# Two-layer AdaLN kernel on one core: modulation products in other pauses of TensorE, transposes between projection halves, gate floor on two rows, expert weights in another order

## The reference

```python
mod = (_silu(L0_c) @ L0_wmod).reshape(L0_c.shape[0], 6, 1, -1)
sa, ca, ga, sb, cb, gb = (mod[:, 0], mod[:, 1], mod[:, 2], mod[:, 3], mod[:, 4], mod[:, 5])
ga = (2 * (ga >= 0) - 1) * jnp.maximum(jnp.abs(ga), 0.25)
gb = (2 * (gb >= 0) - 1) * jnp.maximum(jnp.abs(gb), 0.25)
h = _layernorm(x, axis=-1) * (1 + ca) + sa
x = x + ga * _L0_attn_ref(h, ...)
h = _layernorm(x, axis=-1) * (1 + cb) + sb
x = x + gb * _L0_ffn_ref(h, ...)
...                      # layer 1 the same with its own weights
```

## Time and profile before

| | before |
|---|---|
| median of 3 runs | 437.23 us (436.45 to 443.87) |
| profiled execution | 439.2 us |
| its span, first to last instruction | 437.4 us, 6180 instructions |
| busy share of the span | PE 93%, PEld 70%, DVE 66%, ACT 46%, POOL 30% |
| mean granted TensorE clock | 0.968 of full (2.4 GHz) |
| DMA | 56.89 MB, mean 130 GB/s |

### The profile page before, as it was taken

The page is one execution under the profiler, slowest core; times in us unless marked ns, Lnnn a source line. Parts: engine busy times, 40 slices in busy tenths (PEclk is TensorE's granted clock), DMA queues, the critical chain, the costliest instruction groups (busy, mean ns, idle before and its releaser), DMA issues. The chain is left out here.

```text
span 437.4 us, 6180 instructions
## 1 busy us (share of the span) xinstructions
PE 406.4 (93%) x1923; PEld 305.2 (70%) x1924; DVE 288.4 (66%) x703; ACT 201.9 (46%) x380; POOL 129.3 (30%) x143
## 2 busy tenths in 40 slices
PE   6996898888999999999998899899999979999997
PEld 6553748445777777777776637787677858798887
DVE  4898886997444444444443465989685999985542
ACT  2578825382222222222222238382796488622430
POOL 1000020004777777777777500601000010010000
PEclk9999696988999999999999969999999999999999
DMA  7995766981323233333239249911500000001001
GB/s 262 415 399 132 154 152 178 354 374 43 102 97 104 100 108 96 105 97 109 96 107 275 85 164 377 352 42 25 191 1 0 1 1 0 2 1 45 4 0 49
DMA packets 24010, 56.89 MB, mean 130 GB/s; under 512 B 4528, under 2 KB 15794, under 8 KB 22996
## 3 DMA queue, kind: packets, MB, share of 16 engines
q1 hardware_dynamic: 18564, 41.80, 28.5%
q0 software_dynamic: 5424, 14.82, 10.3%
HBM read 46.10 MB, written 10.50 MB: 129 GB/s over the span
## 5 line engine op out<-in xcount | busy, mean ns | idle before, releaser
L736 PE MATMUL bank<-arena,tile_mem 128*128 x224 | 75.6, 460 | 0.0
L1411 POOL DMA_INDIRECT tile_mem<-h_dram,gidx x57 | 56.0, 982 | 53.8 <-DVE gidx L1789 36.7
L1399 POOL TENSOR_TENSOR rstd<-ve,mhalf 128x2 f32<-128x2 f32 (+1 forms) x14 | 11.3, 806 | 186.3 <-DVE ve L1539 186.3
L1418 POOL DMA_INDIRECT y_dram<-norm,didx x56 | 55.3, 988 | 22.4 <-issue 13.7
L1805 DVE TENSOR_TENSOR tile_mem<-tile_mem,bank 128x176 f32<-128x176 f32 x56 | 18.9, 337 | 62.6 <-ACT tile_mem L1209 62.6
L752 PE MATMUL bank<-arena,tile_mem 88*128 x224 | 57.7, 379 | 0.8 <-DVE tile_mem L1800 0.8
L752 PEld LDWEIGHTS bank<-arena,tile_mem 88*128 88x128 f32 x224 | 42.3, 190 | 15.8 <-issue 1.3
L736 PEld LDWEIGHTS bank<-arena,tile_mem 128*128 128x128 f32 x224 | 38.2, 190 | 11.9
L847 PE MATMUL bank<-x_r,f_r 128*128 128x512 f32 x192 | 44.9, 392 | 0.8 <-DVE x_r L1985 0.7
L1209 ACT ACTIVATE tile_mem<-bank 128x176 f32<-128x176 f32 x56 | 17.8, 317 | 57.8 <-PE bank L736 57.8
L1204 ACT ACTIVATE tile_mem<-bank 128x256 f32<-128x256 f32 x57 | 21.9, 384 | 44.9 <-PE bank L729 44.8
(11 more groups left out here) (286 smaller groups left out, 729.7 us busy)
## 6 DMA issues: line engine op xcount, KB each, us to landing
arena<-w_gu SPq DMA_DIRECT2D x3, 2112.0 KB, 12.4
arena<-w_dn SPq DMA_DIRECT2D x4, 1408.0 KB
arena<-w_gu SPq DMA_DIRECT2D x2, 2464.0 KB, 20.8
arena<-y_dram SPq DMA_DIRECT2D x6, 768.0 KB, 7.8
arena<-w_f SPq DMA_DIRECT2D x6, 512.0 KB, 7.8
arena<-wmod SPq DMA_DIRECT2D x3, 512.0 KB, 9.1
arena<-wmod SPq DMA_DIRECT2D x2, 768.0 KB, 10.8
arena<-y_dram SPq DMA_DIRECT2D x4, 384.0 KB, 4.8
```

The costliest lines, as they stand in the source:

```text
L736: mm = pe.matmul(bank[2 + r % 2][:, 0:2 * M], xgT[r % 2][:, k * P:(k + 1) * P], gu[:, bass.ds(e[k], 2 * M)], start=(k == 0), stop=(k == CT ...
L1411: pool.indirect_dma_start(out=xg[j % 4], out_offset=None, in_=h2_dram, in_offset=bass.IndirectOffsetOnAxis(ap=gidx[:, j:j + 1].bitcast(U32 ...
L1418: pool.indirect_dma_start(out=y_dram, out_offset=bass.IndirectOffsetOnAxis(ap=didx[:, j:j + 1].bitcast(U32), axis=0), in_=yt[j % 4], in_of ...
```

## The change

- The first two pieces of layer 1's modulation products stand behind the two `gated_weights`, the third behind `project(0)`. Their banks become 2, 5, 4, and their waits change with them. `mod_cols` of layer 1 stands ahead of `project(1)`, after a wait for the copy out of bank 2.
- `transposes(B, 0)`, the second norm of sequence 0, stands between the two halves of `project(1)`.
- ACT loads the sigmoid's table ahead of `keep_x(0)`, and `keep_x(1)` stands ahead of `modulated(3, ...)`.
- The floor of layer 0's second gate is applied to the two raw rows (2 x 256) on DVE right behind `exponents(2)`, before they are stored and broadcast, and no more on 128 x 512 ahead of the experts' loop. SP now waits for `gbraw_ready` 2.
- The gate and up weights of experts 17 to 31 are loaded right after `proj_done` reaches B, ahead of the stores of x and h2. Only experts 14 to 16, which lie on X, are loaded after both x stores.

The core of the diff:

```diff
-MOD_BANKS = 4, 7, 4
+MOD_BANKS = 2, 5, 4
...
+        PAST_X = EARLY + -(-NT * C // GUW)
...
-            sp_.wait_ge(gbraw_ready, 1)
+            sp_.wait_ge(gbraw_ready, 2)
             sp_.dma_start(modg_dram, gb_raw).then_inc(mod_out[0], 16)
...
             sp_.dma_start(dn[:, DN_LATE * DNW:E * DNW], w_dn[:, DN_LATE * DNW:E * DNW]).then_inc(dn_in, 16)
+            sp_.wait_ge(proj_done, B)
+            for e in range(PAST_X, E, 5):
+                sp_.dma_start(gu[:, e * GUW:(e + 5) * GUW], w_gu[:, e * GUW:(e + 5) * GUW]).then_inc(gu_late, 16)
...
             sp_.wait_ge(x1_out, 16 * B)
-            for e in range(EARLY, E, 6):
-                sp_.dma_start(gu[:, e * GUW:(e + 6) * GUW], w_gu[:, e * GUW:(e + 6) * GUW]).then_inc(gu_late, 16)
+            sp_.dma_start(gu[:, EARLY * GUW:PAST_X * GUW], w_gu[:, EARLY * GUW:PAST_X * GUW]).then_inc(gu_late, 16)
...
-                    pe.wait_ge(*((sig_ready, CT + 1), (sig_ready, CT + 2), (modrow_ready, 1))[n])
+                    pe.wait_ge(*((exparg_ready, CT + 1), (exparg_ready, CT + 2), (sig_ready, CT + 1))[n])
...
-            def project(b, banks):
+            def project(b, banks, between=None):
 
                 for t in range(TB):
+                    if t == 2 and between:
+                        between()
...
-            for b in range(B):
-                gated_weights(b)
+            gated_weights(0)
+            mod_rows(range(1))
+            gated_weights(1)
+            mod_rows(range(1, 2))
             pe.wait_ge(wg_ready, B)
             preload_x(0, RES_BANKS[0])
             pe.wait_ge(yT_ready, CT)
             project(0, RES_BANKS[0])
-            pe.wait_ge(exparg_ready, CT + 1)
+            mod_rows(range(2, 3))
+            pe.wait_ge(modrow_ready, 1)
             pe.wait_ge(v_used, CT + 1)
             preload_x(1, RES_BANKS[1])
-            mod_rows(range(3))
+            mod_cols((SA, CA, SB, CB), modrow1, 3, 4)
             pe.wait_ge(yT_ready, CT * B)
-            project(1, RES_BANKS[1])
-            mod_cols((SA, CA, SB, CB), modrow1, 3, 4)
+            project(1, RES_BANKS[1], lambda: transposes(B, 0, None, LN2_BANKS[0]))
             pe.wait_ge(route_in, 32)
             for b in range(B):
-                transposes(B + b, b, (x_done, b) if b else None, LN2_BANKS[b])
                 if b:
+                    transposes(B + b, b, (x_done, b), LN2_BANKS[b])
...
+            act.preload_act_table(ACT.Sigmoid)
             keep_x(0)
             modulated(2, 0, 0, SB, CB, LN2_BANKS[0])
...
             token_scores(0)
+            keep_x(1)
             modulated(3, 1, 0, SB, CB, LN2_BANKS[1])
...
             exponents(2)
+            dve.wait_ge(gbraw_ready, 1)
+            gate_floor(gb_raw, gb_tmp[0], gb_tmp[1], gbraw_ready, gb_raw)
             outputs(0)
...
-            dve.wait_ge(modB_in[0], 16 * B)
-            gate_floor(*[v.rearrange("p t c -> p (t c)") for v in (gb0[:, :, :], norm[:, TB:TB + 2, :], norm[:, TB + 2:NT, :])])
-            settle()
```

More of the change, by code:

```diff
@@ L187, in two_layers @@
         modrow1 = tile_mem[0:B, 0:6 * C]
-        gb_raw = tile_mem[0:B, 6 * C:7 * C]
+        gb_raw, *gb_tmp = [tile_mem[0:B, i * C:(i + 1) * C] for i in (6, 7, 8)]
         sh_hid = tile_mem[:, 0:SHT * S].rearrange("p (m n) -> p m n", m=SHT)
@@ L786, in _ @@
             pe.wait_ge(gu_early, 16 * 2)
-            pe.wait_ge(gu_late, 16 * 3)
+            pe.wait_ge(gu_late, 16 * 4)
             pe.wait_ge(dn_in, 16 * 4)
@@ L1153, in _ @@
             token_scores(1)
-            keep_x(1)
             token_rows(1)
@@ L1486, in mod_cols, with gate_floor @@
                 ins.then_inc(modcol_ready, 1)
-            def gate_floor(g, sign, size, done=None):
+            def gate_floor(g, sign, size, done=None, out=None):
                 step(stt(size, g, -1.0, g, ALU.mult, ALU.max))
@@ L1496, in gate_floor @@
                     return step(stt(g, sign, -1.0, size, ALU.add, ALU.mult))
-                stt(size, sign, -1.0, size, ALU.add, ALU.mult).then_inc(done, 1)
+                stt(size if out is None else out, sign, -1.0, size, ALU.add, ALU.mult).then_inc(done, 1)
             def norm_stats(t, src):
@@ L1912, in gated_sums @@
                 pair = slice(ts[0], ts[-1] + 1)
+                if ts[0] == 0:
+                    dve.wait_ge(modB_in[0], 16 * B)
                 dve.wait_ge(csum_done, ts[-1] + 1)
```

## The result

The change made the kernel slower. The median is 449.08 us (448.5 to 451.35, four runs) against 438.75 for the kernel before in the same comparison, a ratio of 1.0232 [1.0189, 1.0274]. The profiled execution took 448.65 us, with a span of 446.8 and a mean granted clock of 0.957 (before 437.4 and 0.968). The forecast was 446.5 us, which is 1.0212 of its base of 437.23, with a range of 443 to 450. The 449.08 lies 2.6 above it, and 1.5 of that is the base, 438.75 here.

The account below looks back on a forecast made before the run. The experts' loop start bounds the kernel, set by DVE's one-hot work, which would now wait for h2 stores behind weights. 8.4 + 0.9 = 9.3 us on 439.2 gives 448.5 profiled, 446.5 as median; range 443 to 450.

Parts of the forecast that it names:

- The first term: DVE's one-hot work waits for the second h2 store, landing at 96.05 instead of 87.6: 8.4 us later, range 7.0 to 10.8.
- The turn: SP's queue: down weights drained by 74.15 before, 2.2 us later after the change, so the moved weights start at 76.35.
- The step on the gate floor: The gate row's store starts at 34.2, lands 35.9; down weights go 2.2 us later, ends 1.2 and 4.2.
- The weights: SP's queue: three moved loads, 5.41 MB at 435 GB/s, take 12.4 us, to 88.75.
- The stores: Behind the weights, three stores take 1.4 us each, 4.2 in all, to 92.95; the second h2 store lands 3.1 later.
- the lower end, 94.6: Earliest landing of the second h2 store: down weights draining only 1.2 us later and 1.2 us for each store.
- The second term: One-hot stretch: TensorE idle about 88 to 97, so half clock at the first shared-expert piece, +0.9 us (-2.1 to +3.0).
- TensorE's order: Moved products and transposes: 2 us gained ahead of DVE's wait, or up to 4 lost at half clock; swallowed either way.
- The gate floor on DVE: Four added operations take 1.6 us in the 2.08 us pause ahead of 34.64; removing those behind `gidx` gives 0.
- 435: Rival: stores don't wait behind the weights, h2 lands before DVE comes, TensorE's 2 us are kept; 435 us, chance 0.08.
- 443.5: Rival: moved weights use the idle DMA share while down weights drain, 1.3 MB or 3.0 us; 443.5 us, chance 0.08.
- 452: Rival: half clock lasts into the experts' loop, doubling TensorE's 5.41 busy us of 104 to 112; 452 us, chance 0.06.

Follow-up runs that it names:

- w_only: The kernel before with only the weight loads of experts 17 to 31 moved ahead of the x and h2 stores; ratio 1.0206, span 446.0 us.
- w_back: The change with its weight loads back behind the x and h2 stores, all other parts kept; ratio 0.9977, span 438.4 us.
- one_load: The change with one weight load (experts 27 to 31, 1.80 MB) ahead of the stores instead of three; ratio 1.0040, span 438.8 us.
- stores_act: The change with both h2 stores issued from ACT's queue, weights still ahead on SP's; ratio 1.0272, span 451.5 us.
- w_back_busy: The change with weight loads behind the stores, plus unused TensorE products: 12 ahead of `project(1)`, two behind each one-hot group; ratio 0.9948, span 431.9 us.
- busy_gap2: The change with 47 unused matmuls in TensorE's wait for the h2 stores and two behind each group of six one-hot products; ratio 1.0217.

## Why the prediction was right, point by point

**The mechanism was right.** The h2 stores stood behind the weights, the wait that had 6.2 us to spare became the one that sets the loop's start, and the loop moved with it one for one. w_only shows that it suffices, w_back that nothing else is lost, as far as its interval tells, and one_load that it goes by bytes.

**The first term, 8.4, measured 8.6, but out of three sizes that were each off; that they nearly cancel is luck.**

- The turn. The step on the gate floor put the issue of the down weights 2.2 later. It came 1.2 later (35.81 against 34.60), as the step's lower end said: the floor ended at 33.77, and the loads followed the row's store by 1.16, less than the 1.7 that I took as the shortest landing. The down weights still ended 2.3 later than before, at 77.26. That is 0.9 behind the 76.35 of the sum. Where the other 1.1 of the 2.3 come from is not shown; in w_only, without the floor, they ended 1.1 later than before too.
- The weights. From there they took 91.2 - 77.26 = 13.9 us, not 12.4, though 0.89 of their 5.41 MB had gone before. The rate was not far off, 420 GB/s in 78 to 88 instead of 435, but rows of the stores ran among theirs from 85.02 on.
- The stores. In return they needed 96.4 - 91.2 = 5.2 us behind the weights, not 4.2 + 3.1 = 7.3; the first of them landed 0.4 after the last weights.

Together +0.9 + 1.5 - 2.1 = +0.3, which puts 96.05 at 96.4. So "one behind the other, each in its time alone" is too sharp: all the bytes together set the end, and the rows mix. Two numbers under it were off as well. The twin store with the 2.7 us was not issued into an empty queue: the first h2 store, issued at 75.25, landed after 3.2, at 78.45, and so ran beside it. And the lower end, 94.6, adds up to 94.5.

The landings keep the order of issue: the weights at 91.2, the second h2 store at 96.4. That agrees with the rule that the forecast went by, in the Trainium skill ("DMA: Bandwidth & Descriptors", section "Queues, rings and completion order"), that each DMA engine takes its descriptors in ring order. The trace does not name the engine of a row, so the order within one engine is not seen.

**The second term, +0.9 for half clock at the first piece, measured +0.94** in DVE's wait and +1.0 in the whole stretch. The place was as put: the first piece took 2.91 instead of 1.98, the second 2.91 as before, the third pair 2.98 where it took 2.84.

**TensorE's order.** The gain of 2 us measured 2.0 (DVE's cast ahead of the wait stands at 85.53 instead of 87.57, the logits 1.56 earlier), and the wait swallowed it, as the step said. Two sizes inside were off. The second projection began 1.5 earlier, at 58.71, not 0.2: with the modulation products in TensorE's pauses, its clock in 42 to 49 was 1.00 instead of 0.63, the first projection began at 47.06 instead of 48.88, and DVE's last output came 1.4 earlier. Against that the half of the projection took 3.78, not 1.86, at the lower clock behind a pause of 2.96; that was the other end that the step named, and it was covered. In w_back, where the cover is gone, the order leads by 2.9 at the one-hot work.

**The gate floor on DVE.** It took 1.36 us (1.6 forecast) in the pause ahead of 34.6, of which 0.80 was left, and the removal behind `gidx` gave nothing: DVE is idle for 3.71 there, the 1.32 of before and 2.4 more.

**The rivals.** The stores waited, so 435 fell; and stores_act shows that not even a queue of their own gives it. The weights did use the idle share, with 0.89 MB ahead of the down weights' end (1.3 MB in the rival), but the second h2 store landed no earlier for it, so 443.5 fell. The loop began at full clock after the change (1.00 in 115.3 to 119.3, and its copies keep their 9.5 to tile 50), so 452 fell here, though in w_back the half clock does reach into the loop, for 1.1 us. Its working has a slip: 5.41 busy us of 8 in 104 to 112, a stretch that is not among rows 7, leave TensorE idle for a third of the time, not for half.

**The sum.** 9.3 us on a span of 437.4 is 446.7, and the profiled span is 446.8. The ratio forecast, 1.0212, lies inside the interval. The interval's lower end, 1.0189, leaves open on which side of 2% it stands, as the near even chances had it.

## What to carry to other kernels

Before a big load is put ahead in a queue, list what stands behind it and how much time each of these has to spare: a load costs its bytes over the rate of the stretch, less that slack, here 4.5 us for each 1.80 MB. A second queue does not save a small transfer whose rows are short beside one whose rows are long; place it ahead, or cut the long rows. A gain ahead of a loop is worth only what still stands at its last tile, so compare one row a tile from the first to the last, and look at the granted clock behind each new gap of TensorE.

## What the runs showed of the hardware that I had not expected

- Two queues shared the DMA engines by packets, not by bytes: 208 and 207 packets in 5 us, 1.87 and 0.21 MB. Stores of 512 KB in rows of 1 KB landed after 19.5 and 21.0 us on a queue of their own beside rows of 14 KB, and after 9.2 and 11.1 beside rows of 1.4 KB.
- A row of a later transfer on the same queue can run before the last row of an earlier one: in the change rows of the x store ran from 85.02 on, the last row of the weights ahead of it from 90.25.
- A full share of the DMA engines was not a full rate: 0.99 and 215 GB/s while rows of the down weights and of the moved weights ran together (66 to 76), 1.00 and 420 GB/s behind them (78 to 88).
- SP was held while it issued: 4.67 us for the second h2 store in the change (0.38 for the first), 20.42 for six loads with short rows. What holds it is not shown.
- Twelve products and two behind each group kept the clock at 1.00 in w_back_busy; 47 and the same two did not in busy_gap2 (0.80), behind a wait of 11 us. What makes the difference was not settled.
